# Block biases added on GpSimd, VectorE and ScalarE instead of by TensorE, and moved casts, masks and a transpose, in a four-stage graph network on Trainium2

## The reference

```python
for i in range(NUM_BLOCKS):                                  # 4
    y = _cond_layer_norm(x, cond, s1_w[i], s1_b[i], b1_w[i], b1_b[i])
    y = _sparse_attention(y, src, dst, wq[i], bq[i], wk[i], bk[i], wv[i], bv[i], wo[i], bo[i])
    x = x + y
    y = _cond_layer_norm(x, cond, s2_w[i], s2_b[i], b2_w[i], b2_b[i])
    y = jax.nn.relu(y @ m_w1[i] + m_b1[i]) @ m_w2[i] + m_b2[i]
    x = x + y
```

## Time and profile before

| | us |
|---|---|
| median of three runs (lowest, highest) | 874.67 (873.52, 875.26) |
| the profiled execution's own time | 874.51 |
| its span, first to last instruction | 873.0 |
| TensorE busy | 835.1 (96%) |
| TensorE weight loads busy | 634.9 |
| VectorE busy | 559.7 (64%) |
| ScalarE busy | 397.5 (46%) |
| GpSimd busy | 230.6 (26%) |
| mean granted clock of TensorE | 0.988 |

### The profile page before, as it was taken

The page is one execution under the profiler, slowest core; times in us unless marked ns, Lnnn a source line. Parts: engine busy times, 40 slices in busy tenths (PEclk is TensorE's granted clock), DMA queues, the critical chain, the costliest instruction groups (busy, mean ns, idle before and its releaser), DMA issues. The chain is left out here.

```text
span 873.0 us, 13200 instructions
## 1 busy us (share of the span) xinstructions
PE 835.1 (96%) x4222; PEld 634.9 (73%) x4223; DVE 559.7 (64%) x1221; ACT 397.5 (46%) x646; POOL 230.6 (26%) x253
## 2 busy tenths in 40 slices
PE   5999789999889999999999999999999998999998
PEld 3666457667577779777787787787786976688786
DVE  7999987748957675676668575774776665720210
ACT  4999893325345622355423364233663235431200
POOL 4000023207431025502226122334013424422200
PEclk9999899999999999999999999999999999999999
DMA  8989915715515653644634446436376467220100
GB/s 189 211 210 235 273 40 125 185 59 133 159 48 125 186 136 109 148 105 137 152 102 135 116 101 199 96 107 150 100 194 176 122 183 202 55 97 1 49 13 36
DMA packets 37845, 113.43 MB, mean 130 GB/s; under 512 B 5908, under 2 KB 6472, under 8 KB 30108
## 3 DMA queue, kind: packets, MB, share of 16 engines
q1 hardware_dynamic: 20604, 79.00, 38.2%
q10 hardware_dynamic: 17184, 33.69, 11.6%
HBM read 105.33 MB, written 7.34 MB: 129 GB/s over the span
## 5 line engine op out<-in xcount | busy, mean ns | idle before, releaser
L690 POOL TENSOR_TENSOR wl<-wraw,wh 128x512 fp32r<-128x512 f32 x140 | 180.2, 1320 | 387.1 <-ACT wh L768 353.4
L1806 PE MATMUL ring<-ohs,ohd 128*128 128x512 f32 x312 | 80.3, 410 | 6.6 <-DVE ohs L1317 6.5
L1806 PEld LDWEIGHTS ring<-ohs,ohd 128*128 128x128 f32 x312 | 59.4, 196 | 31.5 <-issue 18.7
L1295 DVE SCALAR_TENSOR_TENSOR ohd<-iota,dstT,vals 128x256 fp32r x156 | 69.3, 478 | 5.7 <-issue 3.7
L768 ACT ACTIVATE wh<-wraw 128x2048 fp32r<-128x2048 f32 x35 | 66.9, 1911 | 9.5 <-DMA wraw<-in_L_gnn_wk 5.0
L793 ACT ACTIVATE yT_h<-ring 128x512 fp32r<-128x512 f32 x32 | 19.0, 598 | 97.8 <-PE ring L1722 97.8
L817 ACT ACTIVATE ohs<-iota,minus_srcT 128x512 fp32r<-128x512 f32 x78 | 52.3, 713 | 14.1 <-PE ring L1806 7.7
L1733 PE MATMUL mix_ps<-quad,att_shift 120*32 120x512 f32 x384 | 50.3, 603 | 2.3 <-DMA quad<-in_L_gnn_basis 2.3
L695 POOL TENSOR_TENSOR rstd<-ve,half 128x1 f32<-128x1 f32 x44 | 24.1, 549 | 106.5 <-DVE ve L1146 106.3
L1704 PE MATMUL ring<-yT_h,wh 128*128 128x512 f32 x128 | 49.8, 389 | 0.0
L1704 PE MATMUL ring<-yT_l,wh 128*128 128x512 f32 x128 | 49.8, 389 | 0.0
(11 more groups left out here) (390 smaller groups left out, 2151.5 us busy)
## 6 DMA issues: line engine op xcount, KB each, us to landing
quad<-in_L_gnn_basis SPq DMA_DIRECT2D x60, 960.0 KB, 8.5
wraw<-in_L_gnn_m_w ACTq DMA_DIRECT2D x8, 1024.0 KB, 6.3
mix_scratch<-mixed SPq DMA_DIRECT2D x128, 32.0 KB, 4.1
wraw<-in_L_gnn_wv ACTq DMA_DIRECT2D x4, 1024.0 KB, 5.1
wraw<-in_L_gnn_wq ACTq DMA_DIRECT2D x4, 1024.0 KB, 5.5
wraw<-in_L_gnn_wk ACTq DMA_DIRECT2D x4, 1024.0 KB, 5.5
wraw<-in_L_gnn_wo ACTq DMA_DIRECT2D x4, 1024.0 KB, 5.2
wraw<-mix_scratch ACTq DMA_DIRECT2D x4, 1024.0 KB, 5.7
```

The lines of the kernel that those rows point to most:

```text
L690: last = g.tensor_tensor(wl[s][:, k, :], wraw[s][:, k, :], wh[s][:, k, :].bitcast(F32), ALU.subtract)
L1295: return v.scalar_tensor_tensor(out, at.unsqueeze(1).broadcast_to([P, 4, HALF]), dstT[:, e], vals[:, e, :].rearrange("p a b -> p (a b)").u ...
L1806: last = te.matmul(ring[:, banks[b], :], ohd[:, s, b, :], ohs[:, s, :], start=False, stop=False)
```

## The change

- `bv`: broadcast by a load to all 128 rows (`value_bias`); VectorE adds it as it takes the bank, to a plain float32 `vm_raw` (in the place of `vm_l`). ScalarE then copies `vm_raw` to the high part, for all four tiles behind the first query and key, and GpSimd makes the low part.
- `bo`, `m_b2`: broadcast by loads to `row_bias`; GpSimd adds it to the residual `xl` in four instructions, behind the norm that last reads `xl`; `residual` waits for the addition.
- `m_b1`: a third column bias. ScalarE makes relu(bank + b), then a second activation subtracts b from that; VectorE makes the low part as max(bank, -b) less it.
- ScalarE casts W_k behind the copies of `Ta2` and `Ta3` instead of between v0 and v1, in each block.
- In the first block, the casts to `adj` stand behind the cast of W_q, the mask sums behind Ta3's low part, `step_weights` at the last head; the addition to `x` is moved from `first_layer_out` to `first_layer_stats`.
- GpSimd's four low parts of weight 6 are made one ahead of each inverse root instead of four ahead of all.
- The transposes `Tb1` stand in the middle of o3 instead of ahead of the conditioning of tile 2, and VectorE takes them behind that conditioning.

```diff
-    o += [("o", 0), ("o", 1)] + ln("b", 0) + ln("b", 1) + [("o", 2), ("Tb", 0), ("Tb", 1)] + ln("b", 2)
-    o += [("o", 3)] + ln("b", 3) + [("Tb", 2), ("Tb", 3)]
+    o += [("o", 0), ("o", 1)] + ln("b", 0) + ln("b", 1) + [("o", 2), ("Tb", 0)] + ln("b", 2)
+    o += [("Tb", 1), ("o", 3)] + ln("b", 3) + [("Tb", 2), ("Tb", 3)]
...
# SP
-            def load_biases(i):
-                for j, name in ((0, "bv"), (3, "bo"), (4, "m_b1"), (5, "m_b2")):
-                    sp.dma_start(braw[2 * j:2 * j + 2, :], l1[name][bass.ds(i, 1)].broadcast_to([2, D])
-                                 ).then_inc(braw_loaded, 16)
+            def load_value_bias(i):
+                sp.dma_start(value_bias[:], l1["bv"][bass.ds(i, 1)].broadcast_to([P, D])).then_inc(value_bias_loaded, 16)
+
+            def load_row_bias(name, i):
+                sp.dma_start(row_bias[:], l1[name][bass.ds(i, 1)].broadcast_to([P, D])).then_inc(row_bias_loaded, 16)
...
                 load_group(t, 3)
+                sp.wait_ge(row_bias_added, i * (2 * NT) + NT)
+                load_row_bias("m_b2", i)
                 if not last:
-                    sp.wait_ge(brow_ready, i + 1)
-                    load_biases(nxt)
+                    sp.wait_ge(tile_taken, n1.base + i * PER + (n1.at[("v", NT - 1)] + 1))
+                    load_value_bias(nxt)
...
                 load_group(t + 2, 1)
+                if not last:
+                    sp.wait_ge(row_bias_added, i * (2 * NT) + 2 * NT)
+                    load_row_bias("bo", nxt)
                 store_set(t + 1)
...
# GpSimd
-                for j in (1, 2, 3, 4):
+                def add_row_bias(j, after):
+                    pool.wait_ge(row_bias_loaded, i * 32 + (16 * j + 16))
+                    pool.wait_ge(tile_taken, b + (T.at[after] + 1))
+                    for t in range(NT):
+                        g.tensor_tensor(xl[:, t, :], xl[:, t, :], row_bias[:], ALU.add).then_inc(row_bias_added, 1)
+
+                def low_values():
+                    for t in range(NT):
+                        pool.wait_ge(value_hi, i * NT + (t + 1))
+                        g.tensor_tensor(vm_l[:, t, :], vm_raw[:, t, :], vm_h[:, t, :].bitcast(F32), ALU.subtract
+                                        ).then_inc(value_split, 1)
+
+                for j in (1, 2):
+                    low_weight(i * 6 + (W1 + j), j % 3)
+                add_row_bias(0, ("Sa", NT - 1))
+                low_values()
+                for j in (3, 4):
                     low_weight(i * 6 + (W1 + j), j % 3)
                 for t in range(NT):
                     inverse_root(i * 8 + (12 + t), t)
-                for j in (5, 6):
-                    low_weight(i * 6 + (W1 + j), j % 3)
+                low_weight(i * 6 + (W1 + 5), 2)
+                add_row_bias(1, ("Sb", NT - 1))
                 for t in range(NT):
+                    low_weight(i * 6 + (W1 + 6), 0, (t,))
...
# ScalarE
-                def value(t):
-                    hi(("v", t), vm_h[:, t, :])
+                def values():
+                    for t in range(NT):
+                        act.wait_ge(tile_taken, after(("v", t)))
+                        a.activation(vm_h[:, t, :], vm_raw[:, t, :], ACT.Copy).then_inc(value_hi, 1)
+
+                def hidden(m):
+                    hi(("M", m), vm_h[:, m, :], ACT.Relu, bias=column_bias(2, m))
+                    act.wait_ge(hi_ready, i * PERH + (HI1 + hi_of[("M", m)] + 1))
+                    a.activation(vm_raw[:, m, :], vm_h[:, m, :].bitcast(F32), ACT.Identity,
+                                 bias=minus_hidden[:, bass.ds(i * KT + m, 1)]).then_inc(hidden_shifted, 1)
...
                 hwi(1)
-                value(0)
-                hwi(2)
-                value(1)
+                if first:
+                    neighbours()
                 norm_rows("a", 2)
                 norm_rows("a", 3)
-                value(2)
+                hwi(2)
                 query_key(0)
-                value(3)
+                values()
                 lwi(3, after(("v", NT - 1)))
...
# VectorE
                 def value(t):
-                    lo(("v", t), vm_l[:, t, :], vm_h[:, t, :])
+                    ready(T, b, ("v", t))
+                    dve.wait_ge(value_bias_loaded, i * 16 + 16)
+                    v.tensor_tensor(vm_raw[:, t, :], bank(T, ("v", t)), value_bias[:], ALU.add).then_inc(tile_taken, 1)
+
+                def hidden(m):
+                    dve.wait_ge(hidden_shifted, i * KT + (m + 1))
+                    v.scalar_tensor_tensor(vm_l[:, m, :], bank(T, ("M", m)), minus_hidden[:, bass.ds(i * KT + m, 1)], vm_raw[:, m, :],
+                                           ALU.max, ALU.subtract).then_inc(tile_taken, 1)
...
                     if t == 2:
                         transposed("b", 0)
+                    conditioned(T, b, "b", t, nb + t)
+                    if t == 2:
                         transposed("b", 1)
-                    conditioned(T, b, "b", t, nb + t)
...
# TensorE
                     for m in range(NT):
                         done(("PT", h, m))
+                        if h == 0:
+                            pe.wait_ge(value_split, i * NT + (m + 1))
...
-                for t in range(2, NT):
-                    rows_product("o", t, oT_h, oT_l, w, 3)
-                    if t == 2:
-                        mix_in_block(1)
-                        transpose_rows(T, b, "b", 0)
-                        transpose_rows(T, b, "b", 1)
-                    condition(T, b, "b", t, i * 2 + 2)
+                rows_product("o", 2, oT_h, oT_l, w)
+                mix_in_block(1)
+                transpose_rows(T, b, "b", 0)
+                condition(T, b, "b", 2, i * 2 + 2)
+                out = begin(T, b, ("o", 3))
+                part(out, head(3, 0) + head(3, 1), first=True)
+                transpose_rows(T, b, "b", 1)
+                part(out, head(3, 2) + head(3, 3), last=True).then_inc(tile_ready, 1)
+                condition(T, b, "b", 3, i * 2 + 2)
```

More of the change, by code:

```diff
@@ L945, in block_highs @@
                 T = n1_last if last else n1
+                hi_of = hi1_last if last else hi1
                 b = i * PER + n1.base
@@ L1556, in attention_block @@
                 transposed("a", 1)
-                if not first:
-                    split_biases(i)
                 conditioned(T, b, "a", 2, i * 8 + 10)
@@ L1972, in part, with rows_product @@
                     return ins
-                def rows_product(name, t, lh, ll, w, bias):
-                    tile((name, t), [bias_to_rows(bias, brow)] + [p for k in range(KT) for p in
-                         three(cols(lh, k, t), cols(ll, k, t), w[0][:, k, :], w[1][:, k, :])])
+                def rows_product(name, t, lh, ll, w):
+                    tile((name, t), [p for k in range(KT) for p in three(cols(lh, k, t), cols(ll, k, t), w[0][:, k, :], w[1][:, k, :])])
                 def columns_product(name, m, w, rh, rl):
@@ L1984, in value @@
                         done(("Ta", t))
-                    out = begin(T, b, ("v", t))
-                    part(out, [p for k in range(KT) for p in three(cols(yT_h, k, t), cols(yT_l, k, t), w[0][:, k, :], w[1][:, k, :])],
-                         first=True)
-                    if t == 0:
-                        pe.wait_ge(brow_ready, i + 1)
-                    part(out, [bias_to_rows(0, brow)], last=True).then_inc(tile_ready, 1)
+                    rows_product("v", t, yT_h, yT_l, w)
                 def query_key(h):
@@ L2071, in attention_block @@
                 outs[0] = begin(T, b, ("o", 0))
-                part(outs[0], [bias_to_rows(3, brow)] + head(0, 0) + head(0, 1), first=True)
+                part(outs[0], head(0, 0) + head(0, 1), first=True)
                 mix_in_block(1)
@@ L2075, in attention_block @@
                 outs[1] = begin(T, b, ("o", 1))
-                part(outs[1], [bias_to_rows(3, brow)] + head(1, 0) + head(1, 1), first=True)
+                part(outs[1], head(1, 0) + head(1, 1), first=True)
                 done(("PV", HEADS - 2))
@@ L2108, in attention_block @@
                     out = begin(T, b, ("X", t))
-                    part(out, [bias_to_rows(5, brow)], first=True)
                     for k in range(KT):
@@ L2112, in attention_block @@
                             done(("M", k))
-                        end = part(out, three(cols(vm_h, k, t), cols(vm_l, k, t), w[0][:, k, :], w[1][:, k, :]), last=k == KT - 1)
+                        end = part(out, three(cols(vm_h, k, t), cols(vm_l, k, t), w[0][:, k, :], w[1][:, k, :]), first=k == 0, last=k == KT - 1)
                     end.then_inc(tile_ready, 1)
```

100 lines of the change are left out of this document (58 added, 42 removed).

## The result

The changed kernel takes 880.62 us (median of 4 runs, 879.75 to 881.82); the kernel before took 874.10 us on the same chip (4 runs, 872.72 to 875.26). The ratio is 1.007, with a 95% interval of 1.0051 to 1.0089: it is slower by about 6 us. Forecast were 871.0 us and a range of 864 to 876, so the sign was wrong and the time lies above the range.

What follows compares the result with a forecast made beforehand. TensorE, busy nearly the whole span, was taken as the bound. First entry -4.0, later entries +3.3, output projection -1.8, hidden layer and second projection -4.4 sum to -6.9; clock falls add +3.4: 874.51 to 871.0 us, range 864 to 876.

Steps and rivals of the forecast that it cites:

- The removed matmuls: TensorE, all four blocks: 48 bias matmuls of 0.23 us and 32 of 0.12 us go, 14.9 us in all.
- Entry of the first block: Up to the first key product: TensorE's holes shrink, value tile 2 comes 3.8 us earlier, first key at 247.7; gains 4.0 us.
- so both are covered: GpSimd's row-bias additions and value lows, queued behind W_k's lows, cost nothing; uncovered, one instruction of 1.27 us a block.
- Entry of blocks 2 to 4: Before the key product: TensorE waits 2.2 us for W_k's lows behind the later cast; loses 1.1 us, three times, +3.3.
- Output projection, hidden layer and second projection: End of blocks 1 to 3: -0.45 us for the output projection and -1.2 for the other two, each block.
- The clock, two falls more: Behind the new 2.2 us waits: two falls to 1.2 GHz at the four places, 1.7 us each, +3.4.
- The last block: From the last block's PT(0) to the span's end: -0.45 us for the output projection and -0.8 behind it, -1.25.
- The start: Up to the end of the first layers: no change forecast, 0 us.
- The rival on the other side, 882.1 us: GpSimd and VectorE lock each other out, W_k's lows stretch to 1.75 us each, four falls come: 882.1 us; chance 0.10.

Runs made afterwards that it cites:

- before_no_bias_matmuls: The kernel before with the 80 bias matmuls of the four blocks left out, splits and loads kept: 861.36 us, ratio 0.9842 to the kernel before.
- best: Changed kernel with x's addition, Tb1 and later blocks' W_k cast put back, first-block W_k load and cast earlier, x's store behind that load, row_bias cleared: 865.41 us, ratio 0.9886.

## Why the prediction was wrong, point by point

- **The removed matmuls, 14.9 us:** about right. Left out alone they gave 13.8 us, some 12 without a fall that was missing by chance.
- **Entry of the first block, -4.0 (bounds -2.5 and -5.5): this is the step that failed.** It came out at +2.2. The step said "W_k's cast then ends near 241.9": it ended at 247.4. I took the load of W_k as landing when it had before, and did not follow the addition to x, which the change moves on VectorE, to the store on SP that waits for it and to the 1 MB that then travels beside W_k's load. I had written down the three waits that are new on SP and left out the one that was replaced. Undone alone, that is worth 6.3 us by the ratios and 4.1 at PT(0) in the profiles. The 6.2 us between forecast and measured are three pieces: the first key product came 2.7 us late (252.46, less 2.0 of the start, against 247.7); the 4.55 us of work in the fall around it took twice their time, 2.3 more, where the step had left the clock as before; and TensorE waited 1.2 us before PT(0) for VectorE, whose work on the scores begins with that key.
- **Behind it, +1.2 us between PT(0) and PT(1):** "so both are covered" was wrong in the first block. TensorE waited 1.3 us for VectorE's lows of the second head's query and key, and VectorE had come late from the late key and from its split of condition weights, which ran beside GpSimd's value lows and had been undisturbed before. How much of it is the contention was not isolated.
- **Entry of blocks 2 to 4, +1.1 each:** right, +1.2 without the falls, with the wait at 2.17 us against 2.2.
- **Output projection, hidden layer and second projection, -1.65 a block:** -1.1 to -1.2. The second activation keeps pace as forecast but delays the last tile, 0.56 us a block that was not in the sum; the new place of Tb1, forecast to cost nothing, costs 0.36.
- **The clock, two falls more, +3.4:** the net count was right by luck. There are three more in the blocks, which the sum had left at two, and one less in the first layers, which it had not considered and which TensorE spent waiting. Together they cost 4.0 us, 0.6 in block 1 and 3.4 in blocks 3 and 4.
- **The last block, -1.25:** -3.2. A wait for basis data in the next layer (2.26 us) shrank to 0.73, which is 1.5 of the 2.0 us. It isn't simply that work which arrives later finds its data there: the wait is 1.4 us in before_no_bias_matmuls, 14 us earlier, and 2.1 in best, 9 us earlier. Its cause stays open.
- **The start, 0:** +2.0, not foreseen and not explained.

From -3.5 to +5.6 us on the span, the differences are, each with the falls in its stretch (those of blocks 3 and 4 are the forecast's 3.4): first entry +6.2, start +2.0, heads of block 1 +1.2, three block ends +1.5, entries +0.2, last block -2.0. The rival on the other side, 882.1 us, gave nearly the time that was measured, but that is luck, its mechanism is not there: GpSimd's lows took 5.0 us as forecast, not 7, and taking its bias additions away changed nothing.

What it would take to keep part of the gain is one line: with the cast of W_k ahead of the copies in blocks 2 to 4, the change is 4 us faster than before; with x's addition back as well, 9 us.

## What to carry to other kernels

When a change moves an instruction, list every wait whose semaphore it increments, also one that only takes a new name, and follow each to the transfer behind it and to what that transfer then runs beside. A cast that feeds a slow second engine (here 5 us of lows) belongs ahead of short copies that feed a fast one; one line in such an order cost 10 of the 12 us that the removed matmuls were worth. And before a step is moved into an idle gap, ask what buffer it frees: the gap may be filled and the next load late.

## What the runs showed of the hardware that I had not expected

- The load of 1 MB took 5.1 us with neither of the two others beside it (5.2 in best); 6.4 before, beside a basis load of 0.96 MB issued 6.2 us ahead, with the store already in; and 10.2 with the store and the basis load issued 2 us ahead.
- Waits of 1.6 us left the clock at 2.4 GHz in three cases of three; the same wait at 2.17 us was followed by 3.41 us at 1.2 GHz in seven of nine. In block 2 no fall came with the key product at 374.68 or at 370.79, and one came with it at 372.65, behind the same wait.
- GpSimd's lows took 1.25 us each (5.00 for four) behind the late cast of block 2 and 1.48 us (11.86 for eight) beside VectorE's work on masks and conditioning in the first block.
- At the start, while some 500 pieces of 4 bytes landed, the 16 DMA engines moved 1 GB/s at a busy share of 0.09 for over 2 us in one family of kernels, and 186 GB/s at 0.95 in the other, with the same issues at the same times.
